# Two graph layers on one core: x and the adjacency matrix turned by DMA in place of TensorE

## What is computed

```
# layer 0
output = feature @ weight ; q = feature @ wq ; k = feature @ wk
alpha = einsum('bno,bmo->bnm', q, k)
alpha = max(alpha, 0) * (graph != 0)
alpha = softmax(alpha, axis=1)
x = layernorm(x + einsum('bnm,bmo->bno', alpha, output))
# layer 1: 16 heads of 32
q, k, v = heads(x @ Wq + bq), heads(x @ Wk + bk), heads(x @ Wv + bv)
scores = q k^T * 32**-0.5, -inf where mask == 0 ; attn = softmax(scores)
x = layernorm(x + (attn v) @ Wo + bo)
```

## Time and profile before

| | |
|---|---|
| median of three runs | 2968.55 us |
| span of the profiled execution | 2967.6 us |
| TensorE busy | 2902.2 us, 98% |
| VectorE busy | 2365.3 us, 80% |
| ScalarE busy | 2016.6 us, 68% |
| GpSimd busy | 582.6 us, 20% |
| mean granted TensorE clock | 0.992 of full speed |
| moved by the DMA queues | 188.06 MB, mean 63 GB/s |

### The profile page before, as it was taken

The page is one execution under the profiler, slowest core; times in us unless marked ns, Lnnn a source line. Parts: engine busy times, 40 slices in busy tenths (PEclk is TensorE's granted clock), DMA queues, the critical chain, the costliest instruction groups (busy, mean ns, idle before and its releaser), DMA issues. The chain is left out here.

```text
span 2967.6 us, 65967 instructions
## 1 busy us (share of the span) xinstructions
PE 2902.2 (98%) x24264; PEld 1775.5 (60%) x24264; DVE 2365.3 (80%) x4627; ACT 2016.6 (68%) x6414; POOL 582.6 (20%) x1289
## 2 busy tenths in 40 slices
PE   7899999999999999999999999999999999999996
PEld 4565666656666656666666666666666666666554
DVE  4588888888888788888788888888888888888886
ACT  3476676666676766676767766767776766776665
POOL 1121122121122121121121221121221211221210
PEclk9999999999999999999999999999999999999997
DMA  3222122222122222122221122221122221222220
GB/s 121 61 72 76 43 56 73 57 76 72 37 65 61 69 76 62 40 72 54 76 76 54 48 72 54 76 76 47 51 76 54 76 76 42 57 71 59 75 53 24
DMA packets 96369, 188.06 MB, mean 63 GB/s; under 512 B 18608, under 2 KB 34992, under 8 KB 96048
## 3 DMA queue, kind: packets, MB, share of 16 engines
q1 hardware_dynamic: 96048, 183.84, 23.3%
HBM read 49.55 MB, written 33.55 MB: 28 GB/s over the span
## 5 line engine op out<-in xcount | busy, mean ns | idle before, releaser
L647 ACT ACTIVATE e<-sm,nmax 128x128 f32<-128x128 f32 x2048 | 791.1, 391 | 27.6 <-DVE nmax L776 25.6
L598 ACT ACTIVATE qk<-front,bqk 128x512 f16<-128x512 f32 x256 | 175.9, 687 | 381.6 <-PE front L429 381.6
L825 POOL TENSOR_TENSOR ln<-ln 128x1 f32<-128x1 f32 x256 | 49.0, 192 | 1890.2 <-DVE ln L804 1496.6
L647 ACT ACTIVATION_READ_ACCUMULATOR e<-sm,nmax 128x1 f32 x2048 | 391.0, 191 | 0.0
L664 DVE SCALAR_TENSOR_TENSOR pT<-pt_bank,pT 128x512 f16<-128x512 f32 x512 | 348.9, 681 | 42.6 <-ACT pT L653 42.1
L653 ACT ACTIVATE pT<-pt_bank 128x512 f16<-128x512 f32 x512 | 302.8, 591 | 103.6 <-PE pt_bank L543 101.6
L776 DVE TENSOR_REDUCE nmax<-sm 128x4 f32<-128x512 f32 x512 | 351.3, 686 | 17.7
L429 PE MATMUL fin_bank<-W_O,oT 128*128 128x512 f16 x1536 | 356.3, 382 | 1.4 <-DVE oT L664 1.4
L429 PE MATMUL front<-W_V,yT 128*128 128x512 f16 x1536 | 354.0, 380 | 0.0
L429 PE MATMUL front<-xT,W_A 128*128 128x512 f16 x1536 | 353.6, 380 | 0.3 <-DVE xT L664 0.3
L429 PE MATMUL front<-yT,W_Q 128*128 128x512 f16 x1536 | 352.2, 379 | 1.6 <-DVE yT L664 1.6
(11 more groups left out here) (111 smaller groups left out, 4482.3 us busy)
## 6 DMA issues: line engine op xcount, KB each, us to landing
q_st<-qk SPq DMA_DIRECT2D x384, 128.0 KB, 2.4
k_st<-qk SPq DMA_DIRECT2D x384, 128.0 KB, 2.4
x_sb<-in_x SPq DMA_DIRECT2D x128, 256.0 KB, 3.4
out_x<-z_sb SPq DMA_DIRECT2D x128, 256.0 KB, 2.5
adj_i<-in_adj SPq DMA_DIRECT2D x32, 256.0 KB, 4.6
y_sb<-in_L_gnn_wq SPq DMA_DIRECT2D x1, 1024.0 KB, 5.6
yb<-in_L_gnn_wk SPq DMA_DIRECT2D x1, 1024.0 KB, 8.1
x_p<-in_L_gnn_weight SPq DMA_DIRECT2D x1, 1024.0 KB, 10.5
```

The lines of the kernel that those rows point to most:

```text
L598: i = act.activation(dst, src, ACT.Identity, bias=bias, scale=scale)
L647: act.activation(e1[:, k % 2, h, :], sm[:, k % SM_BUFS, h, :], ACT.Exp, bias=nmax[:, k % SM_BUFS, h:h + 1], accum_out=esum[:, n % 2, head: ...
L825: pool.tensor_tensor(ln[:, 8:9], ln[:, 7:8], ln[:, 8:9], ALU.add).then_inc(moments, 1)
```

## The change

`xT` and `adjT` become transposing DMA transfers that SyncE issues. The split x_parts of a group and the transposes of its parts now belong to the pass before (`AHEAD_STEPS`, age -1), spread over the q and k stage; one transfer turns both parts of one image (128x1024 fp16 into 128x8x128), and one turns the four adjacency matrices at the start of a pass. `x_p` and `xT` are laid out by image for it. The scale of 8 no longer lies on xT but is given to bT when t is evicted. `t` 0 waits for all four transfers (`xT_turned`), and VectorE's part of `alpha` for `adjT_turned`. The two functions of SyncE's own order are replaced by the same walk through the list as on the other engines.

```diff
-        ("xT", 0), ("xT", 1), ("x_parts", 0), ("xT", 2), ("PV", 14), ("adj01", 0), ("pT", 15), ("xT", 3), ("v", 2),
-        ("adjT", 0), ("PV", 15), ("S", 0), ("o", 3),
-
-        ("t", 0), ("x_parts", 1), ("exp", 0), ("S", 1), ("t", 1), ("adjT", 1), ("pT", 0), ("exp", 1), ("S", 2),
-        ("x_parts", 2), ("x_parts", 3), ("t", 2), ("pT", 1), ("S", 3), ("exp", 2), ("oT", 3), ("t", 3), ("exp", 3),
+        ("PV", 14), ("adj01", 0), ("adjT", 0), ("pT", 15), ("v", 2), ("PV", 15), ("S", 0), ("o", 3),
+
+        ("t", 0), ("exp", 0), ("S", 1), ("t", 1), ("pT", 0), ("exp", 1), ("S", 2),
+        ("t", 2), ("pT", 1), ("S", 3), ("exp", 2), ("oT", 3), ("t", 3), ("exp", 3),
...
-        ("q", 3), ("pT", 11), ("S", 14), ("mask_size", 0), ("PV", 10), ("k", 1), ("exp", 12), ("exp", 13),
-        ("PV", 11), ("o", 2), ("S", 15), ("fin", 1), ("residual1", 1), ("k", 2), ("oT", 2), ("k", 3), ("stack", 0),
-        ("pT", 12), ("fin", 2), ("residual1", 2), ("stack", 1), ("exp", 14), ("norm1", 1), ("pT", 13), ("exp", 15),
+        ("q", 3), ("x_parts", 0), ("pT", 11), ("S", 14), ("mask_size", 0), ("PV", 10), ("k", 1), ("exp", 12),
+        ("x_parts", 1), ("xT", 0), ("exp", 13),
+        ("PV", 11), ("o", 2), ("S", 15), ("fin", 1), ("residual1", 1), ("k", 2), ("x_parts", 2), ("xT", 1), ("oT", 2), ("k", 3),
+        ("stack", 0), ("pT", 12), ("fin", 2), ("residual1", 2), ("stack", 1), ("exp", 14), ("norm1", 1), ("x_parts", 3), ("xT", 2),
+        ("pT", 13), ("exp", 15), ("xT", 3),
         ("mask", 0), ("v", 1), ("norm1", 2), ("PV", 12), ("pT", 14), ("PV", 13),
...
+                elif what == "xT":
+                    sp.wait_ge(xlo_ready, count(g, GB, k + 1))
+                    sp.dma_start_transpose(xT[:, k, :, :, :].rearrange("p a t n -> p (a t) n"),
+                                           x_p[:, k, :, :].rearrange("p a d -> p (a d)")).then_inc(xT_turned, 16)
+                elif what == "adjT":
+                    sp.wait_ge(adj01_ready, count(g, 1, 1))
+                    sp.dma_start_transpose(adjT[:, :, :], adj01[:, :, :].rearrange("p b m -> p (b m)")).then_inc(adjT_turned, 16)
...
-                if what == "xT":
-                    if k == 0:
-                        pe.wait_ge(x_loaded, count(g, 16 * GB, 16 * GB))
-                    bank = bank_for(g)
-                    for n in range(GB):
-                        mm = pe.transpose(bank[:, n * P:(n + 1) * P], x_sb[:, n, k * P:(k + 1) * P], ident[:, :])
-                    mm.then_inc(f_full, 1)
-                elif what == "adjT":
...
+                if what == "t":
+                    if k == 0:
+                        pe.wait_ge(xT_turned, count(g, 16 * GB, 16 * GB))
```

More of the change, by code:

```diff
@@ L88, in pass_order @@
         ("PV", 8), ("PV", 9), ("oT", 1), ("exp", 11), ("S", 12), ("pT", 10), ("q", 2), ("norm1", 0), ("S", 13),
[3 rows of a table removed]
[1 row of a table added]
+        ("x_parts", 1), ("xT", 0), ("exp", 13),
+        ("PV", 11), ("o", 2), ("S", 15), ("fin", 1), ("residual1", 1), ("k", 2), ("x_parts", 2), ("xT", 1), ("oT", 2), ("k", 3),
+        ("stack", 0), ("pT", 12), ("fin", 2), ("residual1", 2), ("stack", 1), ("exp", 14), ("norm1", 1), ("x_parts", 3), ("xT", 2),
+        ("pT", 13), ("exp", 15), ("xT", 3),
         ("mask", 0), ("v", 1), ("norm1", 2), ("PV", 12), ("pT", 14), ("PV", 13),
     ]
-FRONT_STEPS = "x_parts xT adj01 adjT t alpha p0 mask_size z g norm0 yT q k stack mask load_next".split()
+FRONT_STEPS = "adj01 adjT t alpha p0 mask_size z g norm0 yT q k stack mask".split()
+AHEAD_STEPS = "load x_parts xT".split()
 def age(what, k):
@@ L104, in age @@
         return int(k == LAST)
+    if what in AHEAD_STEPS:
+        return -1
     if what in FRONT_STEPS:
@@ L109, in age @@
     return 1 + int((what, k) in LATE_ATTENTION)
-def order(lo, hi):
-    return [step for step in pass_order() if lo <= age(*step) <= hi]
 def drain_order():
@@ L135, in drain_order @@
     return out
-JOBS = [step for step in pass_order() if step[0] in ("xT", "adjT", "t", "alpha", "v", "z", "g", "yT", "q", "k")]
-HI_JOBS = [step for step in JOBS if step[0] not in ("adjT", "alpha", "g")]
+JOBS = [step for step in pass_order() if step[0] in ("t", "alpha", "v", "z", "g", "yT", "q", "k")]
+HI_JOBS = [step for step in JOBS if step[0] not in ("alpha", "g")]
 def count(group, per_group, k):
@@ L299, in run_passes @@
         def run_passes(eng, step):
[L302 to L307, removed]
+            for p in range(-1, groups):
+                for what, k in pass_order():
+                    if 0 <= p - age(what, k) < groups:
+                        step(what, k, (None, p - age(what, k)))
             for what, k, n in drain_order():
@@ L331, in front_bank @@
         def front_bank(at, *job):
-            assert len(JOBS) % len(fbank) == 0
-            place = (None, 0) if is_at(at, 0) else (None, groups) if is_at(at, groups) else (None, 1)
-            return fbank[job_number(place, job) % len(fbank)]
+            return fbank[job_number(at, job) % len(fbank)]
         def v_pass(g, k):
@@ L367, in _ @@
             sp.dma_start(bo_all[:, :], bo.rearrange("(a d) -> a d", a=1).to_broadcast([P, D])).then_inc(bias_loaded, 16)
[L369 to L420, removed]
+            def step(what, k, g):
+                if what == "load":
+                    if not is_at(g, 0):
+                        sp.wait_ge(f_free, jobs_done(before(g, 1), "g", GB - 1))
+                    for b in range(GB):
+                        sp.dma_start(x_sb[:, b, :], x_d[g[1]][b, :, :]).then_inc(x_loaded, 16)
+                    wait(sp, adj01_ready, count(g, 1, 0))
+                    sp.dma_start(adj_i[:, :, :], adj_d[g[1]]).then_inc(adj_loaded, 16)
+                elif what == "xT":
[5 more added lines that the diff above has]
+                    sp.dma_start_transpose(adjT[:, :, :], adj01[:, :, :].rearrange("p b m -> p (b m)")).then_inc(adjT_turned, 16)
+                elif what == "stack":
+                    dst, parts = ((q_st, (HI, LO, HI)), (k_st, (HI, HI, LO)))[k]
+                    sp.wait_ge(f_free, jobs_done(g, "qk"[k], KT - 1))
+                    wait(sp, s_full, count(g, STEPS, 0))
+                    for r in range(4):
+                        for row, part in enumerate(parts):
+                            sp.dma_start(dst[row * DH:(row + 1) * DH, r, :, :],
+                                         qk[r * DH:(r + 1) * DH, k, part, :, :]).then_inc(stacked[k], 16)
+                elif what == "norm1":
+                    sp.wait_ge(out_ready, count(g, GB, k + 1))
+                    sp.dma_start(out_d[g[1]][k, :, :], z_sb[:, k % 2, :]).then_inc(out_stored[k % 2], 16)
@@ L421, in _ @@
+            run_passes(sp, step)
             for n in range(2):
@@ L697, in step @@
                     dve.tensor_scalar(adj01[:, :, :], adj_i[:, :, :], 0, None, ALU.not_equal).then_inc(adj01_ready, 1)
[L698 to L703, removed]
                 elif what == "t":
-                    front_lo(bT[:, LO, k, :], bT[:, HI, k, :])
+                    front_lo(bT[:, LO, k, :], bT[:, HI, k, :], X_SCALE)
                 elif what == "alpha":
@@ L708, in step @@
                     dve.wait_ge(f_full, jobs_done(g, what, k))
[L709 removed]
+                    dve.wait_ge(adjT_turned, count(g, 16, 16))
                     dve.scalar_tensor_tensor(out=two(e0[:, pair, :]), in0=front_bank(g, what, k)[:, 0:2 * P], scalar=0.0,
```

34 lines of the change are left out of this document (13 added, 21 removed), and 2 rows, old and new, of the table LATE_ATTENTION.

## The result

The changed kernel takes 3183.3 us (median of four runs, 3182.43 to 3185.96) where the kernel before takes 2968.4 beside it: a ratio of 1.0725, 95% interval [1.071, 1.074]. It is 215 us slower. The forecast was 3140, with a range of 3015 to 3300. The profiled execution has a span of 3184.2 us.

The account below looks back on a forecast made before the run. TensorE, busy for 98% of the span, was taken to bound the kernel. To 2967.6 us came 31 passes x (3.89 for the late t 0 + 1.5 for the clock) + 5 at the start, forecast 3140, range 3015 to 3300.

Parts of the forecast that it names:

- The bound: TensorE, busy for 98% of the span, bounds the kernel; a step taken off it is worth its slot.
- the slots: On TensorE, sixteen transposes of x and four adjT products take 1.98 us a pass, 63 us over 32 passes.
- the filler: Twelve of the sixteen transposes only fill TensorE's time between PV 13 and PV 14; 0.66 us a pass comes back.
- SyncE's queue: Transposes of x ahead of and behind the q and k stacks make t 0 4.00 us late, 3.89 net a pass.
- I: Time for which one 256 KB transpose holds SyncE's queue, taken as 1.25 us, with bounds from 0.53 to 3.5.
- The clock: TensorE's clock falls after its waits at the pass boundary, t 0 runs slowly: 1.5 us a pass in all.
- The second prediction: TensorE's clock falls at the PV 14 wait in each pass, as at the last pass boundary before; priced at nothing.
- The sum: 31 passes x (3.89 + 1.5) + 5 = 172 us, added to the profiled span of 2967.6: 3139.6.
- The start: In pass 0, t 0 moves from 39.25 to 43.0 us, with the clock 5 us late.
- Cheap transfers: Rival: one transpose holds SyncE's queue 0.53 us and the clock holds; t 0 1.85 late, about 3025 us; chance 0.12.
- Block by block: Rival: a transpose works through eight 128x128 blocks, holding SyncE's queue 3.5 us; about 3355 us; chance 0.13.
- Hidden after all: Rival: transposes move beside the stacks on SyncE's queue, up to 0.66 us a pass comes back, 2948 us; chance 0.09.

Follow-up runs that it names:

- e1_early: The changed kernel with the splits and transposes of x moved up by 9 to 20 us, all ahead of the store of norm1 0: 2962.4 us, ratio 0.9981.
- e10_two_images: e4_behind with two transposes of two images each (128x2048) in place of four of one image (128x1024): 3146.0 us, ratio 1.0603.
- e4_behind: The changed kernel with the first two transposes of x moved behind the k stack, so that all four stand there: 3161.4 us, ratio 1.0648.
- e5_from_act: The changed kernel with all transposes issued from ScalarE's queue, the last of x after pT 14 and adjT after t 1: 3083.5 us, ratio 1.0392.
- e7_keep_clock: The changed kernel with twelve extra, overwritten products ahead of t 0's wait in each pass but the first: 3155.3 us, ratio 1.0633.

## Why the prediction was right, and where it was off

**The bound, the slots and the filler: right.** That of the removed slots only 0.66 us a pass come back is what e1_early shows (88.97 us a pass against 89.65). Their sum was read too small, 1.98 for 2.17 us, which changed nothing, since the difference lies in the twelve that were filler. PV 14 waits 1.54 us, in all 31 passes. That nothing of TensorE's waits for ScalarE, GpSimd or adjT anew holds too.

**SyncE's queue: right in kind, 1 us short.** In the times of the kernel before (S 15 of the pass shown laid on the one before it, 82.90 us earlier):

| | predicted | measured |
|---|---|---|
| one transpose holds the queue | 1.25 | 1.30 |
| q stack starts | 1085.75 | 1085.92 |
| k stack takes | 8.3 | 8.66 (mean of 30 passes 7.99) |
| k stack ends | 1101.55 | 1102.20 |
| last transposes issued | 1104.55 | 1105.55 |
| t 0 starts | 1106.35 | 1107.30 |
| t 0 later than before | 4.00 | 4.95 |

No term is far off; they lean the same way. The store took 0.59 instead of 0.5, each hand-over on the queue 0.03 to 0.1 us that I hadn't counted, the two transposes 2.67 instead of 2.5. I chose the duration of a copy between SBUF tensors for I (twelve q copies in 7.50 us), and that neighbour was the right one: the store's 0.53 would have given half. That it came so near is partly luck. The reason given was that a transfer costs by its bytes, and by that rule the adjacency's transpose, with half of them, would hold the queue for 0.63 us; it holds it for 1.23.

**The clock: the size was off, and one of the two falls did not come.** The t group took 59.6 us more, 1.9 a pass over 31, where the sum had 1.5; in other passes t 0 took 4.97 us. The second prediction, a fall at PV 14 in each pass, was wrong: v 2 ran at full clock in the pass shown (2.75 us behind a wait of 1.54) and in the others (its group takes 352.3 us, 354.0 before), and e1_early, which has that wait alone, has 71 us at the lower clock against 50 of the kernel before. The row from the last boundary was one case and not the rule: in e1_early the same fall is seen in 5 of 31 passes. It cost the sum nothing, since that fall had been priced at nothing.

**The sum.** Predicted 5.39 a pass; measured, from one q stack to the next, 96.45 on average over 16 distances, against 89.61: 6.8. The queue has 1.0 of the difference and the clock 0.4: 31 x 1.4 = 43 us, which is the distance from 3140 to 3183. The queue's part is that of the average and not only of the pass shown. Over the 30 boundaries after the first two, t 0 starts 26.73 us behind the start of S 15 (25.6 to 28.3), and 21.69 before: 5.04 late. The k stack is shorter there than predicted (7.99), but the q stack takes 7.83 for 7.5, and t 0 starts 2.16 us behind the last issue where the landing was put at 1.8. The start cost 5.2 us by the block g 3 (78.03 against 72.81 us), 5 predicted.

**The rivals.** Cheap transfers fell with 1.30 us a transfer. Block by block fell as well: a whole image is issued in 1.30 us and lands in 2.9. The page of the Trainium skill that gives 1309 ns for one 128x128 block (VectorE: DVE Perf Modes, the three transpose paths) doesn't disagree if this is the time of one transfer alone; here a transfer of four blocks held the queue for 1.23 us and one of eight for 1.30, so it may not be multiplied by blocks. The other page of the Trainium skill, DMA: Bandwidth & Descriptors, with 261 GB/s for a DMA transpose in its table of latencies, fits: two transposes of 512 KB in 3.74 us of issue (e10_two_images) are 280 GB/s, and transposes of 256 KB in a row give 205 (e4_behind's window, the engines busy for 91% of it). It would have given I as 1.0 us; the queue is held 0.3 us longer. Hidden after all fell: the transposes do fill the engines (0.91 of them in e4_behind's window), beside the stacks both land later (e5_from_act), and no margin was there.

## What to carry to other kernels

A transfer that replaces work on the bound engine has to be placed on its own queue's timetable: write down, in order, what stands on that queue between the event that releases it and the consumer, and add up issues and landing; 0.5 us of slack behind 24 copies was the whole budget here, and four more transfers overran it by 5 us. The same transfers 9 to 20 us earlier cost nothing that shows. And work taken off the bound engine gives its slot back only if something else can stand there: the steps removed may have been the filler of another chain, and the gain appears only when the order is made again for the new set of steps.

## What the runs showed of the hardware that I had not expected

- A DMA transpose moves its data in small packets. The page of e5_from_act, where the transposes have a queue of their own (packets, MB, share of 16 engines' span):

```profile
q10 hardware_dynamic: 152576, 37.77, 8.1%
```

  That is 248 bytes a packet. They fill the engines all the same: transposes of 256 KB in a row keep them busy for 91% of a window, at 205 GB/s (e4_behind).
- The hold of the issuing queue is nearly flat for small ones: 1.23 us for 128x512, 1.30 for 128x1024 (fp16), 1.9 each for two of 128x2048.
- A transpose on another queue doubles the landing of plain copies beside it, 2.4 to 4.9 us (e5_from_act).
- Useless matmuls in a wait can pay: 28 us in e7_keep_clock, since TensorE then starts t 0 at its higher clock (2.76 us for 4.43).
- Open: how the 115 us of e5_from_act divide between the shared engines and ScalarE's own queue, and whether another order with the transposes on TensorE would close the 12 us that its idle time allows.
